# A two-layer graph network on one Trainium2 core: in the last stage, each output store waits for a signal from the gathers of three chunks later

## What is computed

```python
h = jnp.maximum(_layernorm(x), 0.0)
x = x + attention(h, Wq, bq, Wk, bk, Wo, bo, src, dst)      # layer 0: softmax over the edges of a node
h = jnp.maximum(_layernorm(x), 0.0)
# layer 1, the last stage here:
agg = segment_sum(h[src], dst, 3125)
ah  = agg / in_deg[:, None]
out = x + h @ W1.T + b1 + ah @ W2.T + b2
```

## Time and profile before

| | us |
|---|---|
| median of 3 runs | 2044.97 |
| lowest and highest run | 2038.87 and 2068.82 |
| span of the profiled execution | 2055.2 |
| PE busy over the span | 1634.7 (80%) |
| DVE busy | 1427.3 (69%) |
| POOL busy | 1110.8 (54%) |

### The profile page before, as it was taken

One profiled execution on the slowest core, in us unless ns is written; L12 is line 12 of the kernel. 1 busy time (PEld: TensorE's weight loads), 2 busy tenths in 40 slices (PEclk: granted clock), 3 DMA queues, 4 the chain that ended last, 5 costly groups with the idle time before them and its releaser, 6 DMA issues.

```text
span 2055.2 us, 23478 instructions
## 1 busy us (share of the span) xinstructions
PE 1634.7 (80%) x5301; PEld 1039.7 (51%) x5301; DVE 1427.3 (69%) x2551; ACT 1155.5 (56%) x3820; POOL 1110.8 (54%) x1346
## 2 busy tenths in 40 slices
PE   5999837887787887778778887863888888788888
PEld 2444426666666666666666664431444444334444
DVE  7999848778777777777877773671556666546664
ACT  3554356887887877868878782330333433233333
POOL 0000057677676776776767722346466666646661
PEclk9999969889989889888988889976898899899999
DMA  8222275545545545555455418546466767756762
GB/s 191 90 91 90 90 217 147 162 151 159 173 132 158 170 139 157 157 155 159 144 164 171 143 49 204 151 135 192 135 200 200 200 201 201 202 158 195 200 200 87
DMA packets 133316, 324.76 MB, mean 158 GB/s; under 512 B 42024, under 2 KB 42274, under 8 KB 133160
## 3 DMA queue, kind: packets, MB, share of 16 engines
q0 software_dynamic: 70240, 229.93, 38.2%
q1 hardware_dynamic: 62920, 93.17, 16.8%
HBM read 283.86 MB, written 39.16 MB: 157 GB/s over the span
## 4 chain that ended last, share of the span: by engine, by line
PE 29%; DVE 26%; issue 21%; another core or an unknown queue 13%; ACT 4%; DMA 4%; DVEq 1%; POOL 1%; SPq 0%; ACTq 0%; POOLq 0%
PE wide L855 12%; PE sums L911 6%; DVE nodes L1411 5%; PE wide L940 5%; DVE nodes L1402 3%; DVE late_rows L1527 2%; ACT heads L776 2%; DMA h2tab<-node 2%; PE sums L1012 2%; DVE ohT L1310 2%; ACT wide L781 1%; DVE nodes L1359 1%; PE wide L850 1%; PE wide L868 1%
## 5 line engine op out<-in xcount | busy, mean ns | idle before, releaser
L697 ACT ACTIVATE nodes<-arena,nodes 128x64 f32<-128x64 f32 x2840 | 684.3, 332 | 7.2 <-issue 4.7
L541 POOL DMA_INDIRECT arena<-ktab,idx x425 | 413.5, 973 | 270.7 <-DVEq L1406 146.6
L911 PE MATMUL sums<-nodes,oh 128*125 128x260 f32 x1768 | 495.4, 425 | 69.2 <-DVE nodes L1359 69.2
L541 POOL DMA_INDIRECT late_rows<-h2tab,idx x425 | 403.6, 950 | 244.8 <-issue 138.0
L855 PE MATMUL wide<-w_sb,node 128*125 128x512 f32 x1000 | 490.9, 635 | 28.8 <-ACT node L767 14.4
L911 PEld LDWEIGHTS sums<-nodes,oh 128*125 128x125 f32 x1768 | 360.2, 209 | 143.0 <-DVE nodes L1359 77.6
L940 PE MATMUL wide<-q_win,ohT 125*128 125x512 f32 x850 | 315.3, 502 | 57.7 <-DVEq L1410 54.9
L1402 DVE TENSOR_TENSOR nodes<-wide,arena 128x1024 f32<-128x1024 f32 (+1 forms) x225 | 258.8, 1160 | 113.5 <-PE wide L940 50.2
L855 PEld LDWEIGHTS wide<-w_sb,node 128*125 128x125 f32 x1000 | 195.2, 202 | 257.8 <-issue 236.0
L940 PEld LDWEIGHTS wide<-q_win,ohT 125*128 125x128 f32 x850 | 225.3, 308 | 94.1 <-DVEq L1410 65.3
L1411 DVE TENSOR_REDUCE nodes<-nodes 128x16 f32<-128x1024 f32 (+1 forms) x225 | 256.9, 1151 | 0.0
(11 more groups left out here) (187 smaller groups left out, 1608.5 us busy)
## 6 DMA issues: line engine op xcount, KB each, us to landing
near_lists<-node_tab SPq DMA_DIRECT2D x27, 531.2 KB
q_win<-qtab SPq DMA_DIRECT2D x26, 448.0 KB
qtab<-q_win SPq DMA_DIRECT2D x17, 448.0 KB
arena<-ktab,idx POOLq DMA_INDIRECT x425
late_rows<-h2tab,idx POOLq DMA_INDIRECT x425
h2tab<-node POOLq DMA_DIRECT2D x25, 250.0 KB, 2.9
node<-h2tab SPq DMA_DIRECT2D x26, 224.0 KB
attn_tab<-kept_sums SPq DMA_DIRECT2D x25, 227.5 KB
```

What stands on the lines that cost most here:

```text
L541: gp.indirect_dma_start(into[:, b, t, :], None, tab, bass.IndirectOffsetOnAxis(ap=idx[:, b, t:t + 1], axis=0)).then_inc(s["rows_in"][b][PA ...
L697: last = act.activation(msgs[:, t, h // HH, h % HH * DH:(h % HH + 1) * DH], rows[:, 1 - b, t, h * DH:(h + 1) * DH], ACT.Copy, scale=den_in ...
L911: last = pe.matmul(halves[:, u, :], oh[:, 1 - b, t, :], rhs[side][:, t, u, :], start=t == 0, stop=t == CT - 1)
```

## The change

A new semaphore `gather_rest`. POOL raises it by one in the gathers of each chunk of the last stage, when it comes to part 2 and before it waits for that part's buffer: at that place it has issued parts 0 and 1, which are 7 of the 17 gathers. After its last chunk it adds 3. SP waits in `store_out(n)` for `gather_rest` to reach n + 4, so that the store of chunk n is issued only when POOL has issued parts 0 and 1 of chunk n + 3. The last three stores (n = 22 to 24) wait for the 3 that are added at the end.

```diff
+        REST, REST_AHEAD = 2, 3
...
+        gather_rest = sem("gather_rest")
...
                 hold(sp, "sp", s5["out_ready"], n + 1)
+                hold(sp, "sp", gather_rest, n + REST_AHEAD + 1)
                 for p0, p1 in ROW_SPLIT:
                     sp.dma_start(io["out"][bass.ds(row + p0, p1 - p0), :], nout[p0:p1, b, 0, :]).then_inc(store5, 16)
                 hold(sp, "sp", store5, (n + 1) * (16 * len(ROW_SPLIT)))
...
                 for t in range(first, end):
                     if t == PARTS[PART[t]][0]:
+                        if s is ag and PART[t] == REST:
+                            gp.sem_inc(gather_rest, 1)
                         hold(gp, "pool", s["rows_free"][PART[t]], g + 1)
...
             chunks(gp, count1, lambda g, b, i: gather(ag, h2tab, late_rows[:, :, :, :].bitcast(F32), g, b))
+            gp.sem_inc(gather_rest, REST_AHEAD)
```

## The result

| | kernel before | changed kernel |
|---|---|---|
| median of the runs, us | 2046.80 (4 runs) | 2131.32 (4 runs) |
| lowest and highest | 2038.87 and 2068.82 | 2128.74 and 2133.13 |
| span of the profiled execution | 2055.2 | 2130.0 |
| PE, DVE, POOL busy | 1634.7, 1427.3, 1110.8 | 1622.5, 1425.5, 1121.1 |

The ratio is 1.0426 with a 95% interval of 1.0379 to 1.0472: the change makes the kernel slower, by about 85 us. The prediction had the direction and the range (2070 to 2300), but forecast 2214, twice the loss (169 us against 85).

The account below looks back on a forecast made before the run. No engine was the bound (DVE, PE, POOL under 81% busy), but the order of events: 3.1 + 6 + 2.9 + 1.0 + 6.6 + 14.4 = 34.0 us per chunk, 22 periods 748 against 579, +169, so 2214 us; range 2070 to 2300.

Parts of the forecast that it names:

- 1 signal: POOL's queue, running ahead of its gathers, gives the signal 3.1 us after the chunk's first gathers start.
- 2 store to next load: SP's queue: from the held store's issue to the next `nrow` load's issue, taken as 6 us, bounds 3.45 and 10.6.
- 3 landing: The `nrow` load from issue to landing: taken as 2.9 us, upper bound 3.7 us.
- 4 transposes: PE transposes the loaded rows in 1.0 us.
- 5 signal to ACT: PE's end-of-transposes signal reaches ACT late in a gather burst: taken as 6.6 us, bounds 0 and 9.2.
- 6 copy to next part 0: From ACT's copy through heads, tails, output, column sums and index list to the next chunk's first gathers: 14.4 us.
- rows 10 and 11: Trace rows of the kernel before: PE's product seen by DVE 8.1 us late; ACT copying PE's transposes late, first by 6.6.
- if signals pass freely after 12 us of gathers: One of the prediction's signs of being wrong: PE's signals not getting stuck that long into a gather burst.
- The rival that takes it: Load late, but its transposes' signal reaches ACT without delay: 27.4 us per chunk, +23, 2068 us; chance 0.16 (below 29.1).
- its second form: Same, but PE's second-product signal is stuck until gathers drain: 29.1 us per chunk, +61, 2106 us; no separate chance.
- The stalls of today go away: Longer periods let gathers drain between bursts, removing POOL's 3.2 us pause and DVE's 4.2 us; included in the sum.

Follow-up runs that it names:

- the second profile of this kernel: The changed kernel run again without further edits, on the chips where the kernel before takes 1820 to 1821 us: 1989.52 us, ratio 1.0916.
- e6: The kernel before, unchanged, run for its profile on the chips of the experiments: 1820.35 us.
- part 0 above: The changed kernel with POOL's signal given ahead of the first part of the gathers instead of the third: 1870.93 us, ratio 1.0271.

## Why the prediction was right in its direction and wrong in its size

**The mechanism held.** The load of `nrow` behind the held store is the cause: taken out from behind it, the loss is gone (ratio 0.9994); held alone, it makes a loss (1.0520). Both were run where the kernel before takes 1821 us. For the first comparison, with its 2047, the trace of the changed kernel shows the same wait where the prediction put it, PE ahead of the `node` transposes, but no experiment removed it there.

**The sum, term by term,** for the chunk shown above, from the start of part 0 at 1648.75:

| term | forecast | measured | from | mean of chunks 1 to 22 |
|---|---|---|---|---|
| 1 signal | 3.1 | 3.0 | 1648.75 to 1651.72 | 3.1 |
| 2 store to next load | 6 | 6.8 | 1651.72 to 1658.53 | 6.6 |
| 3 landing | 2.9 | 5.05 | 1658.53 to 1663.58 | 4.3 |
| 4 transposes | 1.0 | 1.1 | length 1.09 | 1.1 |
| 5 signal to ACT | 6.6 | 0.1 | 1664.67 to 1664.79 | 0.1 |
| 6 copy to next part 0 | 14.4 | 14.4 | 1664.79 to 1679.18 | 14.4 |
| sum | 34.0 | 30.4 | 1648.75 to 1679.18 | 29.6 |

The chunk shown is one of the longer ones; the last column is read from the same trace in the same way.

**The step that failed is term 5.** The prediction read rows 10 and 11 as a rule: after some 10 us of unbroken gathers, signals from PE are stuck until the drain. The changed kernel refutes it, by a sign that the prediction had itself named for being wrong ("if signals pass freely after 12 us of gathers"). ACT's copy comes 0.1 us after the transposes, 16 us into a burst, and only waits of up to 3.0 us are left, 14 of them in 22 periods. The kernel before refutes it more plainly in the experiments, where 374 gathers run without a pause and no engine waits for "remote" in the stage. The bound of 0 that the prediction kept for this term was the right one. The rival that takes it, the load late and its transposes in time, gave 27.4 us and 2068; its second form, 29.1 us and 2106, came nearest to the 29.6 and 2131. But its reason, a stuck signal of the second product, is not what happened: terms 2 and 3 were longer.

**Term 3 was bounded wrongly.** It was capped at 3.7 us by the one row of before, and is 5.05 here, 4.3 on average, and 4.9 in the second profile of this kernel (1527.41 to 1532.28). By the Trainium skill, "DMA: Bandwidth & Descriptors", section on the anatomy of one DMA, an estimate was 2.6 us for such a transfer. The page gives its figures for transfers issued by GpSimd, and this load is issued by SP; the trace disagrees with the estimate, 5.05.

**The base was counted wrongly.** The prediction took 23 periods of 25.2 us for 22 of 26.3. With the right count, 22 held periods of 34.0 and the last of 20.0 (chunk 23, whose store is not held, as after: 2083.7 to 2103.7) would be 768 against 579.4, +189 instead of +169. The true loss in the stage is 671.7 less 579.4, 92 us. So the miscount hid 20 us of the sum's excess. The excess itself is 34.0 less 29.6, 4.4 us per chunk, 97 in all: by the means, term 5 was 6.5 too long, and terms 2 and 3 were 0.6 and 1.4 too short.

**That the time fell into the range is in part luck.** With term 5 at 0.1, everything else as forecast, the sum is 27.5 us and the time, counted as the prediction counted, 2071, at the very edge of 2070 to 2300. Terms 2 and 3, each too short, and the wrong count worked against term 5.

**"The stalls of today go away"** was right, and it accounts for a loss of 85 us and not 168: the waits for "remote" of DVE, POOL and ACT's copy are gone. Where there were none to lose, the same change cost 168. In the stage it cost 92 us in the one and 174 in the other, 82 apart, and DVE's starts in the kernel before were 87 us late in all.

**Still open** is why signals are late in the first comparison and in no profile of the experiments. The same kernel takes 2047 us there and 1820 us on three chips here, and not only in this stage: the last stage itself begins 146 us later (1449.4 against 1303.2), with 57 us of waits for "remote" on DVE in the attention stage and none in the experiments. The chip of the first comparison is not on record, so whether the chip is the reason is not shown. That longer pauses between bursts ended the lateness fits both traces of the first comparison, but no experiment tried it, because none showed lateness. What is shown is that stores beside unbroken gathers are not enough to make signals late: the kernel before has both in the experiments (e6), and none is late.

## What to carry to other kernels

A wait put ahead of a transfer holds up all that stands behind it in that queue. Look first at what is next in the queue and who waits for it, and move that ahead: here one load issued a chunk earlier makes the added wait free. Before costing a period, count the instructions of the row that gives it, and bound an unseen landing beside heavy gathers by more than one row. A pattern seen in three places of one trace (late signals) is not yet a rule to build the largest uncertain term on.

## What the runs showed of the hardware that was not expected

**TensorE's clock pays for a wait too.** In the kernel before, in the experiments, the four `node` transposes and the product behind them take 4.46 us until the next chunk:

```profile
1445.52 0.59 PE L993 MATMUL wide<-ident,node 125*128 125x125 f32 x4
1446.45 3.70 PE L855 MATMUL wide<-w_sb,node 128*125 128x512 f32 x8 [0.34 <-ACT node L767]
1449.98 0.28 PE L1003 MATMUL wide<-ones,junk 128*125 128x1 f32 x2
```

In the changed kernel they take 6.14 us (1532.28 to 1538.42), behind 6.20 us in which PE waited. The granted clock (third number from the end of a row; the row begins with the stretch, its length and each engine's busy time, and ends with the busy share of the DMA engines and GB/s) says why, here over the tiles, the wait and the stretch behind it:

```profile
1510.40:1525.00 14.60, 14.60 (x44) 7.88 (x43) 8.82 (x12) 3.24 (x6) 5.58 (x6) 1.00 0.39 112
1525.00:1532.00 7.00, 1.08 (x6) 0.50 (x4) 3.88 (x6) 0.59 (x1) 5.17 (x7) 0.86 0.83 250
1532.00:1538.40 6.40, 6.12 (x12) 3.10 (x13) 1.92 (x4) 4.66 (x7) 4.88 (x6) 0.62 0.77 230
```

It is 1.00 (2.4 GHz) over the tiles and 0.62 behind the wait, that is mostly the 1.2 GHz level: 1.7 us of the 7.9 lost per chunk. In the first comparison the kernel before paid it already (1616.20 to 1622.96, 6.8 us; now 1663.58 to 1670.32, 6.7; 6.1 and 6.2 on average), so it adds next to nothing there. Where the wait was short (0.41 us, part 0 above) the product took 3.60 us.

**POOL's queue runs ahead of its gathers.** In the kernel that holds only the load, the signal behind 11 gathers reached SP at most 5.0 us after the first of them started (1466.70 to 1471.68), when at 1.25 us each only 4 had begun.

**One kernel, one code, two times:** 2047 us in the first comparison, 1820 to 1821 us on three chips of the experiments, with a ratio of 1.04 for the change in the one and 1.09 in the other. What differs between them is not on record. A ratio measured in one place need not hold in the next if the chain that a change lengthens was not the same chain there.
